# A graph network on one core: each indirect scatter made to wait for the one four ahead of it

## The reference

```
h = relu(layernorm(x)); x = x + L0(h)   # 4 steps: messages by edge type, segment sum over dst, GRU
h = relu(layernorm(x)); x = x + L1(h)   # attention over the edges
h = relu(layernorm(x)); x = x + L2(h)   # dst_emb = segment_sum(h[src], dst)
h = relu(layernorm(x)); x = x + L3(...) # segment sum and max of edge_attr by src, then an MLP
```

```
transformed = einsum('nd,khd->knh', feat, W) + b[:, None, :]
a = segment_sum(transformed[etypes, src], dst)
feat = gru_cell(a, feat)
```

## Time and profile before

| | us |
|---|---|
| median of 3 runs | 8854.78 |
| the profiled execution | 8876.89 |
| its span | 8875.0 |
| GpSimd busy | 3692.8 |
| vector engine busy | 4824.9 |
| TensorE matmul busy | 4613.8 |
| first scatter to last scatter | 482.4 to 2818.3 |

### The profile page before, as it was taken

How to read it: one execution, slowest core, us unless ns; L and a number is a source line. 1 busy time by engine, 2 the same in 40 slices (tenths; PEclk the granted TensorE clock), 3 DMA queues, 4 the chain that set the end, 5 groups by cost and what they waited for, 6 DMA issues and landing times. The chain is left out here.

```text
span 8875.0 us, 66244 instructions
## 1 busy us (share of the span) xinstructions
PE 4613.8 (52%) x21729; PEld 2818.2 (32%) x21729; DVE 4824.9 (54%) x9853; ACT 4454.6 (50%) x2943; POOL 3692.8 (42%) x3327
## 2 busy tenths in 40 slices
PE   0110001311113777676385555757839668788866
PEld 0100001100001333333274444546728556211135
DVE  9963346200002777776374333745629446888863
ACT  0000000200002999997385445647929668688855
POOL 0067773677775000000467444274865753000041
PEclk9555555555555888888697777878969879555578
DMA  9710000300101777777296555767829656455566
GB/s 415 340 0 0 0 0 29 94 18 7 33 4 64 298 303 297 303 296 266 90 310 182 150 165 167 231 182 243 307 74 343 222 201 235 177 223 219 217 241 217
DMA packets 523231, 1589.94 MB, mean 179 GB/s; under 512 B 148178, under 2 KB 207929, under 8 KB 493190
## 3 DMA queue, kind: packets, MB, share of 16 engines
q1 hardware_dynamic: 329082, 1408.51, 44.1%
q10 hardware_dynamic: 88332, 146.04, 5.0%
q0 software_dynamic: 105472, 31.16, 2.7%
HBM read 1046.14 MB, written 539.23 MB: 179 GB/s over the span
## 5 line engine op out<-in xcount | busy, mean ns | idle before, releaser
L1016 ACT ACTIVATE full<-ring 128x3136 fp32r<-128x3136 uint8 x731 | 1995.9, 2818 | 793.8 <-remote 469.6
L858 PE MATMUL ps_all<-full,TR 128*128 128x448 f32 x8232 | 1864.9, 383 | 651.1 <-ACT full L1016 248.0
L623 POOL DMA_INDIRECT mat_d<-cT,idxT x1563 | 1660.2, 1062 | 945.0 <-issue 485.2
L666 POOL DMA_INDIRECT two<-in_edge_attr,eid x1029 | 1183.2, 1150 | 1858.4 <-DMA csum_d<-two 1379.0
L858 PEld LDWEIGHTS ps_all<-full,TR 128*128 128x128 f32 x8232 | 1583.3, 196 | 929.5 <-issue 463.1
L809 PE MATMUL ps_all<-ring,T 128*64 128x448 f16 x8232 | 1159.5, 408 | 1377.3 <-issue 993.6
L1030 ACT ACTIVATE ring<-ring 128x3136 uint16<-128x3136 uint8 x197 | 553.4, 2809 | 1268.6 <-remote 1141.5
L809 PEld LDWEIGHTS ps_all<-ring,T 128*64 128x64 bf16 x8232 | 556.0, 124 | 1979.1 <-issue 1409.8
L1469 DVE CAST full<-ring 128x1568 fp32r<-128x1568 uint8 x487 | 478.5, 983 | 966.6 <-remote 451.9
L761 PE MATMUL ps_all<-ident,two 128*128 128x128 f32 x448 | 109.1, 424 | 1275.2 <-DVE two L1174 1113.2
L666 POOL DMA_INDIRECT ring<-in_edge_attr,eid x539 | 608.5, 1129 | 164.3 <-issue 164.3
(11 more groups left out here) (419 smaller groups left out, 6139.2 us busy)
## 6 DMA issues: line engine op xcount, KB each, us to landing
ring<-mat_d SPq DMA_DIRECT2D x784, 784.0 KB
mat_d<-ring SPq DMA_DIRECT2D x98, 1568.0 KB, 39.8
csum_d<-two SPq DMA_DIRECT2D x192, 784.0 KB
two<-csum_d SPq DMA_DIRECT2D x32, 3136.0 KB, 10.2
base_d<-two SPq DMA_DIRECT2D x49, 1568.0 KB
TR<-two_d SPq DMA_DIRECT2D x282, 256.0 KB
C<-csum_d SPq DMA_DIRECT2D x17, 3136.0 KB, 10.2
C<-base_d SPq DMA_DIRECT2D x49, 800.0 KB
```

Of the source, the lines that this page charges most:

```text
L623: pool.indirect_dma_start(mat_d, bass.IndirectOffsetOnAxis(idxT[:, col:col + 1], 0), cT[:, col:col + 1], None).then_inc(s_sc[g % 8], 16)
L666: pool.indirect_dma_start(slab[n % SLABS][:, c, 0:FA], None, attr, bass.IndirectOffsetOnAxis(eid[:, at:at + 1], 0)).then_inc(s_at[n % SLAB ...
L858: mm = pe.matmul(accs[:, j, 0:GW], parts.bitcast(F32R), full[:, m % WIDES, j * GW:(j + 1) * GW].bitcast(F32R), start=first, stop=True, ski ...
L1016: act.activation(to, own, ACT.Copy).then_inc(s_ha, 1)
```

## The change

The eight semaphores of the groups become four (`AFLOAT = 4`), and scatter `k` adds to semaphore `k % 4`. Before scatter `k` GpSimd waits until scatter `k - 4` has landed, as the semaphore then stands at `16 * (k // 4)`. So at most four scatters are under way. The wait for a whole group goes. `s_done` is raised before scatter `a = 4` of the next group instead of `a = 8`. After the last scatter there are four waits, one for each semaphore.

```diff
+AFLOAT = 4
+assert NCOL % GC > AFLOAT or NCOL % GC == 0
-            s_sc = dma_sems(*(t + f"scattered{k}" for k in range(8)))
+            s_sc = dma_sems(*(t + f"scattered{k}" for k in range(AFLOAT)))
-                    if a == GC // 2 and g:
-                        pool.wait_ge(s_sc[(g - 1) % 8], 16 * GC * ((g - 1) // 8 + 1))
+                    if k >= AFLOAT:
+                        pool.wait_ge(s_sc[k % AFLOAT], 16 * (k // AFLOAT))
+                    if a == AFLOAT and g:
                         pool.sem_inc(s_done, 1)
                     col = a * P + g
                     pool.indirect_dma_start(mat_d, bass.IndirectOffsetOnAxis(idxT[:, col:col + 1], 0),
-                                            cT[:, col:col + 1], None).then_inc(s_sc[g % 8], 16)
+                                            cT[:, col:col + 1], None).then_inc(s_sc[k % AFLOAT], 16)
...
-                last = NGC - 1
-                pool.wait_ge(s_sc[last % 8], sum(16 * (min(NCOL, (x + 1) * GC) - x * GC) for x in range(last % 8, NGC, 8)))
+                for k in range(AFLOAT):
+                    pool.wait_ge(s_sc[k], 16 * ((NCOL - 1 - k) // AFLOAT + 1))
                 pool.sem_inc(s_done, 1)
```

## The result

On the chip of the first comparison the changed kernel takes 7786.49 us (median of 4 runs, 7754.56 to 7901.29), the kernel before 8844.66 (8828.69 to 8858.06). The ratio is 0.881, with a 95% interval of 0.875 to 0.888. The predicted time was 8862 us. On other chips the same change costs time: 1.033 (1.031 to 1.035) on chip 7. Both need explaining.

The account below looks back on a forecast made before the run. Step 0 was taken to begin only when GpSimd's scatters end, at GpSimd's own pace. Slow landings added +7 us, x 0.94 = +7, all other terms 0: 8855 + 7 = 8862 us, range 8750 to 8925.

Parts of the forecast that it names:

- Fewer scatters queued: Scatter row: four instead of over eight handed over ahead, about two truly under way in both; TensorE's share unchanged.
- the factor of 0.94: End of scatters: of each 1 us delay there, TensorE uses 0.06 us and 0.94 us is lost.
- Rival D: Step 0: fewer queued scatters set TensorE free beside them; 1250 us saved, 7600 us; chance 0.10.
- The new wait where landing is slow: Scatters beside SP's seven loads, 1593.2 to 1637.8, cost 6 us, later single loads 1; together +7, ends 2 and 40.
- rival A: 1598 to 1638 us, SP's first loads: landings lengthen, wait bites 31 scatters, 62 us; 8913 us; chance 0.17.
- ordinary scatters cost nothing: Quiet stretches: landing takes 2.2 to 3.2 us, so the wait for scatter k - 4 is over before its turn; cost 0.
- the wait for the messages took up what was lost before it: First 672 scatters: slow landings cost at most 44 us, taken up by GpSimd's 171.9 us wait for messages; cost 0.
- Four waits after the last scatter: After the last scatter: four waits in place of one end with the same landing; cost 0.
- the lack of the group wait: GpSimd's scatters: the removed group wait held it only once, ahead of the messages; effect 0.
- The earlier raise of `s_done`: Next group's first scatter landed: `s_done` comes one period later, 1.3 us; cost 0, at most 1.3 once.
- the mark that I gave for D: 1900 to 2000 us: matmuls in hundreds instead of 36 and a granted clock above 0.5 would show D.
- rival C: The 890 scatters: GpSimd keeps the short 1.26 us period instead of 1.372, 100 us less; 8761 us; chance 0.07.

Follow-up runs that it names:

- semaphores alone: Kernel before with eight semaphores, four serving a group in turn, GpSimd still waiting only for whole groups: 6639.5 us, ratio 1.001 on free chip 14.
- the pace behind every second scatter: Kernel before plus one unneeded small GpSimd `tensor_scalar` after every second scatter from 16 on, group wait kept: 7800.3 us, ratio 0.869 on holding chip 10.
- the lighter pace: Kernel before plus one small GpSimd `tensor_scalar` behind every fourth scatter from 16 on, no new landing wait: 8708.8 us, ratio 0.986 on holding chip 11.
- The queue cut: Kernel before plus, from scatter 676 on, a GpSimd memset and a wait for it behind every fourth scatter: 6685.2 us, ratio 1.007 on free chip 14.

## Why the prediction was wrong

- **The step that failed** is "Fewer scatters queued": "The transfers truly under way are 2.2/1.26, about two, in both. So I see no reason that TensorE's share changes." I put this term at 0, and it was worth more than all others: TensorE runs 584 matmuls in 100 us beside the scatters, not 36, and with that the factor of 0.94 fell as well. Two under way holds only in quiet stretches. Where SP loads, landings can take more than four periods (10.9 us at the first wait), the new wait breaks the row and slows it (214.2 us of waits in step 0), and the unbroken row at its full rate is what holds TensorE. Rival D came out, with 1285.5 us less after the last scatter against the 1250 of its price. But not for its reason, a smaller stock: with six and eight afloat the hold stays, and a pace that lets some 16 be handed over ahead lifts it. That its price nearly came is luck: it was worked out for TensorE set free, whatever frees it.
- **"The new wait where landing is slow"** was mis-sized in both of its terms: 6 + 1 us against 214.2 measured after 1598 us. I counted 31 scatters of one spell and took later loads one by one, from a trace in which the held TensorE let SP load once in 88 us. With TensorE free the DMA engines are busy 81% of the time from 1900 to 2000 us, not 6%, and slow landings come in all of step 0. What I had as rival A's mechanism holds throughout, at a mean period of (3023.1 - 1600.9)/889 = 1.600 us instead of 1.372. On a free chip it is all that the change does.
- The Trainium skill, "DMA: Bandwidth & Descriptors", section "Queues, rings and completion order", has engines go round the queues packet by packet. By that rule waits should bite wherever loads run. The trace agrees in the main: 214.2 of the 226.2 us of waits lie in step 0, beside the loads.
- **Right:** ordinary scatters cost nothing: 1388 of them in the changed kernel stand behind "issue", mostly at 0.30 us, though each carries a wait. In the sort nearly nothing moved (24 and 32 matmuls in 400 us), and the wait for the messages took up what was lost before it: 171.9 to 159.9 us. Four waits after the last scatter in place of one show no cost (semaphores alone, 1.001), nor does the lack of the group wait (eight afloat, 1.003, 0.996 to 1.010). The earlier raise of `s_done` wasn't timed by itself.
- **Clock and use:** the mark that I gave for D, matmuls of 1900 to 2000 us in hundreds and a clock above 0.5, is what came (584, 0.88).
- **The pace:** rival C didn't come. Idle time at "issue" in step 0 fell only from 275.9 to 248.6 us, with the scatters that wait for a landing (173 in the whole span) moved to the other kind of wait, and the mean duration rose from 1062 to 1079 ns: no shorter period was won.
- I also took it that the chip isn't part of the question. On a free chip none of the steps about TensorE applies, and the sum that is left is a loss of 210 us.

What the runs show and what is argued: that a row that is broken and slowed frees TensorE, without a new wait for landings, is shown by the pace behind every second scatter, and that a lower limit on the scatters afloat by itself doesn't is shown by six and eight. That the changed kernel stays free because loads keep landings slow, slow landings keep breaking the row, and breaks keep TensorE free to call for loads, is argued. For it speak the executions of the lighter pace that fall into two groups, and six afloat, which broke once in step 0 and then was held.

The runs don't part "a break" from "a lower rate", and on the holding chips the rate by itself orders them all: freed rows have a mean period of 1.57 to 1.62 us in step 0 and of 1.72 and more in the sort, held ones of 1.37 to 1.41. The queue cut, which breaks the row and hardly slows it, would have parted them, but met only free chips. What in the chip the row takes from TensorE, and why some chips show it, isn't known.

The change frees step 0, not the sort ahead of it nor all that lies behind it; it still takes 7786 us on a holding chip and 6852 on a free one. Steps 1 to 3 run beside GpSimd's gathers of edge attributes, and these rows still hold TensorE. The changed kernel on the first chip, then on chip 7, 80 us beside gathers each:

```profile
3920.00:4000.00 80.00, 14.19 (x29) 8.21 (x28) 2.85 (x6) 8.45 (x3) 58.94 (x62) 0.50 0.16 36
3500.00:3580.00 80.00, 71.49 (x339) 62.54 (x338) 55.10 (x125) 77.92 (x29) 64.64 (x51) 1.00 0.91 310
```

29 matmuls beside 62 indirect DMAs, and 339 beside 51 (on the free chip these come every 1.57 us, not every 1.29). From the last scatter to the end it is 4771.2 us on the one and 4000.4 on the other (6847.4 - 2847.0). No run here broke the rows of the gathers.

No version beats both kernels on both kinds of chip. The wait from scatter 673 on keeps the gain (7804.8 us) and costs 1.027 instead of 1.033 on a free chip; there the kernel before is the best. Five afloat, at 1.013, wasn't seen on a holding chip.

## What to carry to other kernels

If another engine issues one instruction to each DMA of GpSimd and waits for nothing that the profile shows, try to break and slow GpSimd's row before anything else: a small instruction of its own behind every second DMA tells in one run, at a price of 3.4% where nothing is held. Time such a change on several chips, since the same program can take 8850 us on one and 6640 on the next, and the sign of the change can turn with it. Size a wait for landings with the load that the change itself brings about, not with the quiet trace of before.

## What the runs showed of the hardware

- On holding chips (the first one, 0, 10 and 11) TensorE gets one matmul and one weight load done in 2.80 us beside an unbroken row of scatters of 1.40 us; on a free one (chip 14) it runs 610 matmuls in 100 us beside 73 scatters, and the times of chips 7, 8 and 15 are of the same kind.
- The traces differ too: those of holding chips hold 38,555 to 47,426 records of landings, those of free chips 85,896 to 86,690, for the same transfers. The freed kernels on holding chips have few as well (38,555 for the changed one, 47,426 for the pace behind every second scatter). What a wait is put down to rests on fewer records there. Every timed run was also recorded, so whether the hold is tied to the recording can't be told.
- Limiting the scatters under way to two costs 11% on a free chip, with 840.4 us of waits: the longest of them is 11.4 us.
- A satisfied wait is free: with six afloat 1557 scatters stand behind "issue" with 478.7 us in all, 0.31 us each, where 1562 had 485.2 us before.
